# Second cross attention: query products in two pairs, values one a step, the routing's logits at step 9 and positions at 22, read at 23

## The chip, the cores and the metric

The kernel runs as one program on one core of a Trainium2 chip. The metric is the device time of one execution in microseconds (us). All data is float32.

## The reference, cut to what matters

Two transformer decoder layers run over 32 sequences of 100 tokens of width 256, with a context of 361 rows of width 128 for each sequence. The stage that the change touches is the cross attention of layer 1, and with it the routing of the mixture of experts that follows:

```python
# L1 cross attention, 16 heads of 64: q = layernorm(x), kv = ctx_512
qh = (q @ Wq).reshape(B, N, 16, 64).transpose(0, 2, 1, 3)
kh = (kv @ Wk).reshape(B, M, 16, 64).transpose(0, 2, 1, 3)
vh = (kv @ Wv).reshape(B, M, 16, 64).transpose(0, 2, 1, 3)
attn = softmax(einsum('bhnd,bhmd->bhnm', qh, kh) / 8)
x = x + einsum('bhnm,bhmd->bhnd', attn, vh) ... @ Wo + bo
# L1 mixture: routing of each token to 8 of 64 experts
scores = sigmoid(layernorm(x) @ gate.T); sfc = scores + e_bias
# 4 of 8 groups by the sum of their two best, then the 8 best experts;
# weights = scores of the chosen ones, divided by their sum, times 2.5;
# position of a token in its expert's list = how many tokens before it chose that expert (capacity 256)
```

## The kernel before

The whole kernel is five stages in a row; the one here is `packed_cross_attention` (layer 1). It handles two sequences (u = 0, 1) in a **turn**. There are 16 turns of real work, written as one turn of preparation (turn -1), turn 0, a hardware loop over turns 1 to 14, and turn 15. A turn is 26 **steps** (`SLOTS`), and each engine runs through the same 26 steps in its own program; semaphores tie them together. The order of the work is written by hand: tables at the top of the function say at which step a piece is issued.

At every step n the Tensor engine (PE) makes one tile of scores, 128 rows (head and token) by 361 keys, for the tile that is 10 steps ahead (`scores`, L1093), and transposes the probabilities of the tile that is 5 steps ahead in three pieces (`turn_probs`, L1100). The Vector engine (DVE) takes the maximum of the new scores (L1247) and divides the tile that is 9 steps ahead by its sum (reciprocal L1252, scaling L1254). The Scalar engine (ACT) copies the transposed probabilities out of PSUM (`move_probs`, L1198) and makes the exponentials (`exponent`, L1203). Work that is 10 steps ahead passes over into the next turn: from step 16 on, the scores are those of the next turn.

Beside this, single pieces have steps of their own:

- `WEIGH_AT`: probabilities times values, 24 pairs of small products (L1114), at steps 3, 9, 16, 22; `Y_AT`: the output projections y0 at step 13 and y1 at step 24 (L1123), which the Vector engine adds to X (`add`, L1259).
- `X_AT`, `P_AT`, `Q_AT`: for the next turn, the transposed input (step 4), four query projections p0 to p3 (L1057) and four query products with the key weights (L1071). Product j fills two PSUM tiles, q0.j and q1.j, which the Scalar engine copies to `qT` (L1185).
- `V0_AT`, `V1_AT`: the values of the sequences 0 (of the next turn) and 1 (of this turn), six products each (L1082), copied by the Scalar engine (L1192).
- The routing of the turn before this one, woven in: `ROUTED_X` (transposed input, PE L763), `ROUTED_L` (logits, PE L782, moved by the Scalar engine in L790), `ROUTED_C` (positions by counting, PE L867 and L868). The choice of the experts (`choose`) is a chain of some 30 small Vector instructions, cut by `yield` into groups; `CHOOSE_AT` says at which steps a group runs. One group reads the positions out of PSUM (L840 to L842); the last one finds the eight row numbers of each token (L853 to L860), and waits before it for the semaphore `rows_free` (L855), that the rows of the turn before were written.
- GpSimd (POOL) then copies the normalised tokens into the rows (`copy_rows`, L876) and sends 16 indirect writes (`send_row`, L882). `PACE` holds each of them back until the Vector engine has reached a given step; the first `FIRST` of them come before GpSimd's two small norm operations (L227) and the bias addition (L1006), the others after.

All the pieces of the list share two PSUM banks, 6 and 7, through `Ring`: the entries of a turn (30 of them) in order of their steps are dealt in turn to bank 6 and bank 7, and the engine that fills an entry first waits until the entry before it in the same bank has been read out:

```python
def plan(self, names):
    self.bank = {name: n % self.n for n, name in enumerate(names)}
...
def wait_free(self, pe, name, i):
    pe.wait_ge(self.moved[self.bank[name]], self.before(name, i) + 1)
```

So moving one entry changes which pairs of entries follow each other in a bank. Before the change the order is, as step:entry(bank), v for values, q for a query product (two entries):

0:v1.0(6) 1:v1.1(7) 2:v1.2(6) 4:xT(7) 4:v1.3(6) 5:p0(7) 6:v1.4(6) 7:p1(7) 8:v1.5(6) 8:rx(7) 10:rl(6) 11:p2(7) 12:p3(6) 13:y0(7) 14:q0.0(6) 14:q1.0(7) 15:q0.1(6) 15:q1.1(7) 17:v0.0(6) 17:rc(7) 18:v0.1(6) 18:v0.2(7) 19:q0.2(6) 19:q1.2(7) 20:v0.3(6) 21:q0.3(7) 21:q1.3(6) 23:v0.4(7) 24:y1(6) 25:v0.5(7)

Here rx, rl and rc are the routing's transposed input, logits and positions.

## Time and profile before

| | us |
|---|---|
| median of 3 runs (3569.85 to 3587.38) | 3585.91 |
| the profiled execution: its own time | 3585.76 |
| its span | 3584.0 |
| Tensor engine busy | 3278.9 (91%) |
| Vector engine busy | 1882.1 (53%) |
| Scalar engine busy | 1653.5 (46%) |
| GpSimd busy | 783.2 (22%) |

The span is what the profiler covers between the first and the last instruction; the profiled execution's own time is 1.8 us longer. In a timeline, a row is an instruction or a few of one kind: its start in us, its length, the engine, the line, the operation, output and inputs, how many, and in square brackets how long the engine had been idle before it and who ended that. An instruction of the Tensor engine's float32 work shows as two in the counts (x2 for one product). Ends of matmuls are modelled and overlap the start of the next one, so the distance from start to start is what an instruction costs.

### The profile page before, as it was taken

How to read it: one execution, taken by the hardware profiler on the slowest of the kernel's cores; microseconds unless marked ns; L12 is line 12 of the kernel's file. 1: busy time of each engine (PE TensorE's matmuls, PEld its weight loads, DVE VectorE, ACT ScalarE, POOL GpSimd, SP SyncE). 2: the span in 40 equal slices, each digit the busy share in tenths (PEclk: the TensorE clock that was granted, in tenths of full speed). 3: DMA queues.
4: the chain of work that ended last, by engine and by line, in shares of the span. 5: the costliest groups of instructions: out<-in, count | busy, mean ns of one | idle time of the engine just before them, and what ended most of it. 6: DMA issues, size and time to landing. Idle time of an engine off the chain costs nothing. (4 is left out here: it accounts for less than half of the span.)

```text
span 3584.0 us, 76477 instructions
## 1 busy us (share of the span) xinstructions
PE 3278.9 (91%) x24554; PEld 2427.9 (68%) x24555; DVE 1882.1 (53%) x5145; ACT 1653.5 (46%) x4616; POOL 783.2 (22%) x854
## 2 busy tenths in 40 slices
PE   5999999899999898999996979999999999979982
PEld 4777776566666566777775757777677777656761
DVE  3555555577777645222224645665656656543333
ACT  2555555576666511222222336666666666631220
POOL 0000000000000000333331100223233232234774
PEclk9999999899999889999998989999999999989996
DMA  8500000300000042111112010100000000113784
GB/s 268 140 0 0 0 0 2 150 10 10 10 10 10 29 137 75 28 29 32 30 21 51 0 51 10 33 26 21 15 11 13 13 12 15 40 49 106 216 209 138
DMA packets 136402, 181.21 MB, mean 51 GB/s; under 512 B 36156, under 2 KB 108601, under 8 KB 135308
## 3 DMA queue, kind: packets, MB, share of 16 engines
q1 hardware_dynamic: 81810, 131.61, 11.9%
q0 software_dynamic: 45760, 26.67, 4.6%
q10 hardware_dynamic: 8762, 22.01, 1.7%
q8 instruction: 42, 0.69, 0.1%
q14 instruction: 28, 0.23, 0.0%
HBM read 116.11 MB, written 103.61 MB: 61 GB/s over the span
## 5 line engine op out<-in xcount | busy, mean ns | idle before, releaser
L1247 DVE TENSOR_REDUCE e_nmx<-PS 128x1 f32<-128x361 f32 x416 | 221.5, 532 | 400.5 <-PE PS L1093 350.9
L1093 PE MATMUL PS<-e_cT,e_qT 128*128 128x361 f32 x832 | 337.6, 488 | 0.0
L1599 ACT ACTIVATE b_p<-PS,b_nmx 100x361 f32<-100x361 f32 x512 | 267.6, 569 | 149.5 <-DVE b_nmx L1681 149.5
L882 POOL DMA_INDIRECT slot_rows<-r_row,r_rows_now x256 | 256.4, 1002 | 360.4 <-DVE e_p L1254 306.6
L1198 ACT ACTIVATE e_pT<-PS 121x384 f32<-121x384 f32 (+1 forms) x416 | 199.1, 479 | 221.1 <-PE PS L1100 212.4
L2592 PE MATMUL PS<-c_wgu,c_tile_xT 128*128 x912 | 290.0, 461 | 1.2 <-ACT c_tile_xT L2647 1.2
L1100 PEld LDWEIGHTS PS<-ident,e_p 128*121 128x121 f32 x1248 | 199.6, 186 | 105.8 <-issue 10.4
L1681 DVE TENSOR_REDUCE b_nmx<-PS 100x1 f32<-100x361 f32 x512 | 243.8, 526 | 45.6 <-PE PS L1445 45.6
L1203 ACT ACTIVATE e_p<-PS,e_nmx 128x361 f32<-128x361 f32 x416 | 232.7, 559 | 37.0 <-DVE e_nmx L1247 36.9
L1452 PEld LDWEIGHTS PS<-ident,b_p 100*121 100x121 f32 x1536 | 188.2, 185 | 63.0 <-ACT b_pT L1583 32.8
L1452 PE MATMUL PS<-ident,b_p 100*121 100x100 f32 x1536 | 223.0, 280 | 8.4 <-ACT b_pT L1583 6.2
L2592 PEld LDWEIGHTS PS<-c_wgu,c_tile_xT 128*128 128x128 f32 x912 | 169.5, 191 | 77.9 <-issue 2.8
L2848 POOL DMA_INDIRECT sum<-f_y,f_y_token x128 | 199.5, 1559 | 89.1 <-issue 55.2
L1100 PE MATMUL PS<-ident,e_p 128*121 128x128 f32 x1248 | 206.0, 275 | 9.0 <-issue 9.0
L1093 PEld LDWEIGHTS PS<-e_cT,e_qT 128*128 128x128 f32 x832 | 143.5, 191 | 97.6 <-issue 87.5
L1082 PE MATMUL PS<-e_wv,e_cT 128*121 128x512 f32 x384 | 198.9, 601 | 11.4 <-DVE r_key L842 11.3
L517 ACT ACTIVATE a_sm<-a_sm,a_nmx 100x100 f32<-100x100 f32 x512 | 186.0, 368 | 13.9 <-DVE a_nmx L585 13.9
L1254 DVE TENSOR_SCALAR e_p<-e_p,e_rden 128x361 f32<-128x361 f32 x416 | 170.4, 410 | 14.8
L1686 DVE COPY b_pT<-PS 121x300 f32<-121x300 f32 x256 | 120.0, 469 | 95.2 <-PE PS L1452 91.2
L2654 ACT ACTIVATE c_gated<-PS 128x352 f32<-128x352 f32 x114 | 52.9, 464 | 232.5 <-PE PS L2592 231.8
L2612 PE MATMUL PS<-c_wd,c_hT 128*128 x684 | 157.2, 379 | 0.7 <-DVE c_hT L2683 0.7
L1114 PE MATMUL PS<-e_pT,e_v 121*64 121x100 f32 x3072 | 147.3, 252 | 0.4 <-ACT e_pT L1198 0.4
(339 smaller groups left out, 6490.1 us busy)
## 6 DMA issues: line engine op xcount, KB each, us to landing
f_w<-in_f_W SPq DMA_DIRECT2D x64, 384.0 KB
slot_rows<-a_empty SPq DMA_DIRECT2D x1, 21504.0 KB, 65.0
f_xg<-slot_rows SPq DMA_DIRECT2D x64, 336.0 KB
c_wgu<-in_c_GU ACTq DMA_DIRECT2D x8, 1408.0 KB, 16.6
sum<-X SPq DMA_DIRECT2D x2, 3200.0 KB, 57.2
f_sums<-sum SPq DMA_DIRECT2D x16, 400.0 KB
b_cT<-in_ctx_T SPq DMA_DIRECT2D x32, 181.5 KB, 2.3
e_cT<-in_ctx_T SPq DMA_DIRECT2D x32, 181.5 KB, 2.4
```

Of the source, the lines that this page charges most:

```text
L882: pool.indirect_dma_start(out=self.rows, in_=self.row[:, u, :], in_offset=None, out_offset=bass.IndirectOffsetOnAxis(ap=self.rows_now[:, u ...
L1082: mr.fill_done(pe.matmul(mr.at(v_name, KEYS, 512), cT[:, u, c * KEYS:(c + 1) * KEYS], wv[:, n * 512:(n + 1) * 512], start=True, stop=True) ...
L1093: sr.fill_done(pe.matmul(sr.at(f"s{m}", ROWS, CTX), qT[:, at:at + ROWS], cT[:, u, 0:CTX], start=True, stop=True), f"s{m}")
L1100: last = pe.transpose(tr.at(f"p{m}", KEYS, CH, ROWS)[:, c, :], p[:, m % NP, c * KEYS:(c + 1) * KEYS], k.ident[:])
L1198: tr.move_done(act.activation(pT[:, :, at:at + rows], tr.at(f"p{m}", KEYS, CH, ROWS)[:, :, 0:rows], ACT.Copy), f"p{m}")
L1203: sr.move_done(act.activation(p[:, m % NP, 0:CTX], sr.at(f"s{m}", ROWS, CTX), ACT.Exp, bias=nmx[:, m:m + 1], accum_out=den[:, m:m + 1]), f ...
L1247: dve.tensor_reduce(nmx[:, m:m + 1], sr.at(f"s{m}", ROWS, CTX), AX.X, ALU.max, negate=True).then_inc(max_ready, 1)
L1452: last = pe.transpose(tr.at(f"p{g}{a}", KEYS, CH, S)[:, c, :], p[:, g % 2, a, c * KEYS:(c + 1) * KEYS], k.ident[0:S, 0:S])
L1599: sr.move_done(act.activation(p[:, g % 2, a, 0:CTX], sr.at(f"s{g}{a}", S, CTX), ACT.Exp, bias=nmx[:, g, a:a + 1]), f"s{g}{a}")
L1681: dve.tensor_reduce(nmx[:, g, a:a + 1], sr.at(f"s{g}{a}", S, CTX), AX.X, ALU.max, negate=True).then_inc(max_ready, 1)
L2592: last = pe.matmul(banks.at(f"{a}{n}", 128, HALF), xT[:, c, :], wgu[:, bass.ds(now, 1), what, c, n * HALF:(n + 1) * HALF] .rearrange("p o ...
L2848: pool.indirect_dma_start(out=k.sums[n % 2].rearrange("s b d -> (s b) d"), in_=y[:, n % 4, half, :], in_offset=None, out_offset=bass.Indir ...
```

## The change

It edits tables and the order of three things:

- The query projections are at steps 5 to 8 in a row. The query products come as two pairs, at steps 10 and 11 and at steps 17 and 18. No step has two values products any more; v1.4 and v1.5 go to steps 12 and 14.
- The routing's logits are issued at step 9 (before: 10), its positions at step 22 (before: 17). The choice of experts runs at steps 12, 13, 16, 18, 20, 22, 23, 24 and 25 in nine groups: a new `yield` cuts the group that finds the eight best experts. The positions are read at step 23 and the last group runs at step 25.
- `add(1, i)` stands inside step 25, ahead of the last group of the choice. GpSimd's writes are paced by steps 1, 2 and 4 to 17 of the next turn (before: 22 to 25 and 3 to 14), two of them ahead of the norms (before: four).

The stage after this one (`shared_and_experts`) gets one more call of `next` at its step 4, so that the choice of the last turn keeps its places.

```diff
@@ class Routing, choose
         for u in range(2):
             last = dve.max(self.best8[:, u, :], masked[:, u, :])
         link(last)
+        yield
         dve.sem_inc(self.passed, 1)
@@ packed_cross_attention
-    P_AT = {5: 0, 7: 1, 11: 2, 12: 3}
-    Q_AT = {14: 0, 15: 1, 19: 2, 21: 3}
-    V0_AT = {17: (0,), 18: (1, 2), 20: (3,), 23: (4,), 25: (5,)}
-    V1_AT = {0: 0, 1: 1, 2: 2, 4: 3, 6: 4, 8: 5}
-    ROUTED_X, ROUTED_L, ROUTED_C = 8, 10, 17
-    CHOOSE_AT = (12, 13, 14, 15, 16, 18, 19, 20)
-    FIRST = 4
-    PACE = [22, 23, 24, 25] + [SLOTS + n for n in range(3, 15)]
+    P_AT = {5: 0, 6: 1, 7: 2, 8: 3}
+    Q_AT = {10: 0, 11: 1, 17: 2, 18: 3}
+    V0_AT = {15: 0, 19: 1, 20: 2, 21: 3, 23: 4, 25: 5}
+    V1_AT = {0: 0, 1: 1, 2: 2, 4: 3, 12: 4, 14: 5}
+    ROUTED_X, ROUTED_L, ROUTED_C = 8, 9, 22
+    CHOOSE_AT = {12: 1, 13: 1, 16: 1, 18: 1, 20: 1, 22: 1, 23: 1, 24: 1, 25: 1}
+    FIRST = 2
+    PACE = [SLOTS + n for n in (1, 2, *range(4, 18))]
@@ the Vector engine's turn
-                        if prev and n in CHOOSE_AT:
-                            next(choosing, None)
-                    if this:
-                        add(1, i)
+                        if this and n == SLOTS - 1:
+                            add(1, i)
+                        if prev:
+                            for _ in range(CHOOSE_AT.get(n, 0)):
+                                next(choosing, None)
@@ shared_and_experts
-    CHOOSE_AT = {2: 1, 3: 2, 4: 1, 5: 1, 6: 1, 7: 2}
+    CHOOSE_AT = {2: 1, 3: 2, 4: 2, 5: 1, 6: 1, 7: 2}
```

The entries of the two banks now follow each other like this:

0:v1.0(6) 1:v1.1(7) 2:v1.2(6) 4:xT(7) 4:v1.3(6) 5:p0(7) 6:p1(6) 7:p2(7) 8:p3(6) 8:rx(7) 9:rl(6) 10:q0.0(7) 10:q1.0(6) 11:q0.1(7) 11:q1.1(6) 12:v1.4(7) 13:y0(6) 14:v1.5(7) 15:v0.0(6) 17:q0.2(7) 17:q1.2(6) 18:q0.3(7) 18:q1.3(6) 19:v0.1(7) 20:v0.2(6) 21:v0.3(7) 22:rc(6) 23:v0.4(7) 24:y1(6) 25:v0.5(7)

Two places of the Tensor engine's program and one of the Vector engine's show it. Rows are instructions in program order; those without an output are register and wait instructions; "waits" names the semaphores, `bank6_moved` being the count of entries read out of bank 6. Lines of the changed kernel are one higher or one lower than those of the kernel before.

The Tensor engine in the loop, from y0 (step 13) on, before:

```order
L1123 MATMUL PS<-e_wo,e_oT 100x256 [waits bank7_moved]
L1123 MATMUL PS<-e_wo,e_oT 100x256 x7
L87 REGISTER_ALU
L1093 MATMUL PS<-e_cT,e_qT 128x361 [waits bank0_moved]
L87 REGISTER_ALU
L1098 REGISTER_ALU [waits bank4_moved]
L1100 MATMUL PS<-ident,e_p 121x128 [waits e_scaled]
L1100 MATMUL PS<-ident,e_p 121x128 x2
L159 REGISTER_ALU [waits bank7_moved]
L159 REGISTER_ALU [waits bank6_moved]
L1071 MATMUL PS<-e_short,e_wkT 128x200 [waits bank7_moved]
```

The same place now:

```order
L1124 MATMUL PS<-e_wo,e_oT 100x256 [waits bank6_moved]
L1124 MATMUL PS<-e_wo,e_oT 100x256 x7
L87 REGISTER_ALU
L1094 MATMUL PS<-e_cT,e_qT 128x361 [waits bank0_moved]
L87 REGISTER_ALU
L1099 REGISTER_ALU [waits bank3_moved]
L1101 MATMUL PS<-ident,e_p 121x128 [waits e_scaled]
L1101 MATMUL PS<-ident,e_p 121x128 x2
L159 REGISTER_ALU
L1083 MATMUL PS<-e_wv,e_cT 121x512 [waits bank7_moved]
```

Before, a query product stood one step behind y0 and needed the bank of y0; now a values product in the other bank stands there, and the next user of y0's bank is v0.0 at step 15.

The Tensor engine in the loop at the positions (step 17) and the two values products of step 18, before:

```order
L867 MATMUL PS<-r_taken,earlier 100x64
L868 MATMUL PS<-r_before,ones 100x64
L87 ISA
L1093 MATMUL PS<-e_cT,e_qT 128x361 [waits bank2_moved]
L87 REGISTER_ALU
L1098 REGISTER_ALU [waits bank4_moved]
L1100 MATMUL PS<-ident,e_p 121x128 [waits e_scaled]
L1100 MATMUL PS<-ident,e_p 121x128 x2
L159 REGISTER_ALU
L1082 MATMUL PS<-e_wv,e_cT 121x512 [waits bank6_moved]
L159 REGISTER_ALU
L1082 MATMUL PS<-e_wv,e_cT 121x512 [waits bank7_moved]
```

The positions now (step 22), up to the values product of step 23:

```order
L868 MATMUL PS<-r_taken,earlier 100x64
L869 MATMUL PS<-r_before,ones 100x64
L87 REGISTER_ALU
L1094 MATMUL PS<-e_cT,e_qT 128x361 [waits bank1_moved]
L87 REGISTER_ALU
L1099 REGISTER_ALU [waits bank3_moved]
L1101 MATMUL PS<-ident,e_p 121x128 [waits e_scaled]
L1101 MATMUL PS<-ident,e_p 121x128 x2
L159 REGISTER_ALU
L1083 MATMUL PS<-e_wv,e_cT 121x512 [waits bank7_moved]
```

The next user of the positions' bank was the second values product one step later; it is now y1, two steps later.

The Vector engine in the loop at the last group of the choice (step 25) now, up to its first wait for the rows:

```order
L1246 TENSOR_REDUCE e_nmx<-PS 128x1 [waits bank0_filled,r_step]
L105 REGISTER_ALU
L1251 RECIPROCAL e_rden<-e_den 128x1 [waits bank2_moved]
L1252 REGISTER_ALU
L1253 TENSOR_SCALAR e_p<-e_p,e_rden 128x361 [waits e_rden_ready]
L1258 ISA [waits bank6_filled]
L1258 TENSOR_TENSOR X<-X,PS 100x256
L854 MAX r_key<-r_key 100x8 x2
L241 REGISTER_ALU
L857 TENSOR_SCALAR r_row<-r_score 100x2x64 [waits r_rows_free,r_step]
L858 TENSOR_SCALAR r_row<-r_token_f 100x2
```

Before, this group stood at step 20, between two steps of plain softmax work; now it follows the addition of y1 and stands ahead of the next turn's first maximum.

## Rows read from the trace of the kernel before

**Rows 1.** Busy time by engine (count), Tensor clock, DMA share, GB/s: one turn.
```profile
2497.60:2563.34 65.74, 63.45 (x469) 47.06 (x468) 40.03 (x150) 41.06 (x109) 19.48 (x22) 1.00 0.06 16
```
**Rows 2.** Timeline of SP: the routing's store, once a turn, turns 2 and 14.
```profile
2300.39 0.60 SPq L774 DMA_DIRECT2D r_xT_rows<-r_xT  x1
...
3089.25 0.56 SPq L774 DMA_DIRECT2D r_xT_rows<-r_xT  x1
```
**Rows 3.** Groups by line, 14 turns: busy, mean ns | idle before, releasers.
```profile
L1082 PE MATMUL PS<-e_wv,e_cT 128*121 128x512 f32 x338 | 174.2, 597 | 11.3 <-DVE r_key L842 11.3
...
L1071 PE MATMUL PS<-e_short,e_wkT 64*128 64x200 f32 x448 | 53.1, 355 | 20.8 <-DVE X L1259 17.0 <-ACT e_v L1192 3.7
```
**Rows 4.** Timeline of PE, steps 14 and 15 of one turn.
```profile
2511.11 0.49 PE L1100 MATMUL PS<-ident,e_p 128*121 128x128 f32 x3
2512.82 0.95 PE L1071 MATMUL PS<-e_short,e_wkT 64*128 64x200 f32 x8 [1.22 <-DVE X L1259]
...
2514.41 0.49 PE L1100 MATMUL PS<-ident,e_p 128*121 128x128 f32 x3
2514.83 0.95 PE L1071 MATMUL PS<-e_short,e_wkT 64*128 64x200 f32 x8
```
**Rows 5.** Timeline of DVE: the addition of y0 in that turn.
```profile
2512.36 0.41 DVE L1259 TENSOR_TENSOR X<-X,PS 100x256 f32 x1
```
**Rows 6.** Timeline of PE: the two values products of step 18.
```profile
2522.61 1.02 PE L1082 MATMUL PS<-e_wv,e_cT 128*121 128x512 f32 x2
2524.44 1.12 PE L1082 MATMUL PS<-e_wv,e_cT 128*121 128x512 f32 x2 [0.81 <-DVE r_key L842]
```
**Rows 7.** Timeline of DVE: the last of three reads of the positions.
```profile
2524.09 0.29 DVE L842 TENSOR_SCALAR r_key<-PS 100x128 f32<-100x128 f32 x1
```
**Rows 8.** Timeline of PE, step 21: the last query product.
```profile
2529.80 0.49 PE L1100 MATMUL PS<-ident,e_p 128*121 128x128 f32 x3
2530.56 0.95 PE L1071 MATMUL PS<-e_short,e_wkT 64*128 64x200 f32 x8 [0.27 <-ACT e_v L1192]
```
**Rows 9.** Timeline of ACT: copies of query products (two each) and of values.
```profile
2513.80 0.90 ACT L1185 ACTIVATE e_qT<-PS 128x400 f32<-128x400 f32 x2 [1.12 <-PE PS L1071]
...
2515.86 0.90 ACT L1185 ACTIVATE e_qT<-PS 128x400 f32<-128x400 f32 x2
...
2529.92 0.59 ACT L1192 ACTIVATE e_v<-PS 121x512 f32<-121x512 f32 x1
...
2544.92 0.60 ACT L1192 ACTIVATE e_v<-PS 121x512 f32<-121x512 f32 x1
```
**Rows 10.** Timeline of PE: values at steps 25 and 0, with no wait.
```profile
2542.00 1.02 PE L1082 MATMUL PS<-e_wv,e_cT 128*121 128x512 f32 x2
2542.86 0.77 PE L1093 MATMUL PS<-e_cT,e_qT 128*128 128x361 f32 x2
...
2543.79 1.02 PE L1082 MATMUL PS<-e_wv,e_cT 128*121 128x512 f32 x2
```
**Rows 11.** Timeline of DVE: last group's start (step 20), y1's addition, step 0's maximum.
```profile
2529.76 0.35 DVE L853 MAX8 r_key<-r_key 100x8 f32<-100x64 f32 x2
...
2542.84 0.41 DVE L1259 TENSOR_TENSOR X<-X,PS 100x256 f32 x1
2543.67 0.53 DVE L1247 TENSOR_REDUCE e_nmx<-PS 128x1 f32<-128x361 f32 x1 [0.42 <-PE PS L1093]
```
**Rows 12.** Single lines over the span: ns min/median/max, first and last start.
```profile
L876 POOL COPY r_row<-r_xn x16: 607/609/612, 2267.8 to 3230.5; 100x512 f32<-100x512 f32 x16
...
L882 POOL DMA_INDIRECT slot_rows<-r_row,r_rows_now x256: 985/992/1143, 2271.6 to 3251.5; - x128
...
L1254 DVE TENSOR_SCALAR e_p<-e_p,e_rden x416: 406/408/523, 2137.6 to 3181.5; 128x361 f32<-128x361 f32 x139
```
**Rows 13.** Timeline of PE in turn 15: after the loop's exit, and at the positions.
```profile
3155.71 1.00 PE L1100 MATMUL PS<-ident,e_p 128*121 128x128 f32 x3 [8.99 <-issue]
...
3181.47 0.45 PE L867 MATMUL PS<-r_taken,earlier 100*100 100x64 f32 x2 [2.14 <-DVE r_before L830]
```

More of the change, by code:

```diff
@@ L950, in packed_cross_attention @@
         order += [(n, 2, f"q{r}.{j}") for n, j in Q_AT.items() for r in range(HT)]
-        order += [(n, 3, f"v0.{m}") for n, ms in V0_AT.items() for m in ms]
+        order += [(n, 3, f"v0.{m}") for n, m in V0_AT.items()]
         led = [name for _, _, name in order]
@@ L1143, in turn @@
                         if nxt and n in V0_AT:
-                            for m in V0_AT[n]:
-                                values(0, m, i + 1)
+                            values(0, V0_AT[n], i + 1)
                         if this and n in V1_AT:
@@ L1227, in turn @@
                         if nxt and n in V0_AT:
-                            for m in V0_AT[n]:
-                                move_values(0, m, i + 1)
+                            move_values(0, V0_AT[n], i + 1)
                         if this and n in V1_AT:
```

## The prediction

> **What bounds the kernel now.** I read the busy table of single turns first. In a turn of 65.74 us the Tensor engine is busy for 63.45 at clock 1.00 (the upper of its two levels, 2.4 GHz), the Vector engine for 40.0, the Scalar engine for 41.1 and GpSimd for 19.5 [rows 1]. So the Tensor engine sets the pace of this stage, and only what makes it stand still is to be had; all its products stay the same in number. Then the timeline of SP shows that the turns are equal: its store comes once a turn, and from the one at 2300.39 to the one at 3089.25 are twelve turns, 788.86 / 12 = 65.74 us [rows 2]. One turn can stand for the 14 of the loop. Then the groups by line, over 14 turns: the Tensor engine is idle ahead of three pieces alone. It waits 17.0 us for the addition of y0, 11.3 us for the read of the positions and 3.7 us for a copy of values [rows 3], 32.0 us in all, 2.3 us a turn.
>
> Last, the timelines of one turn tell why, and what each costs from start to start.
>
> - **First wait, step 14.** The transposes start at 2511.11; the query product behind them would start 0.42 later, as it does one step on (2514.41 to 2514.83), so at 2511.53. It starts at 2512.82, **1.29 us late** [rows 4]: its bank held y0, and the addition of y0 began at 2512.36 [rows 5]. The bank opened 0.46 us after that start.
> - **Second wait, step 18.** A values product takes 0.86 us (2542.00 to 2542.86), the scores and transposes of the next step 0.93 (to 2543.79), so a plain step with values is 1.79 [rows 10]. The first of step 18 starts at 2522.61, so the second was due at 2523.47 and came at 2524.44, 0.97 late [rows 6]. What follows a wait also runs 0.1 us longer (1.12 against 1.02), which makes **1.07 us**. It waited for the Vector engine's third read of the positions, which began at 2524.09 [rows 7]; the bank opened 0.35 us after that start.
> - **Third wait, step 21.** The query product comes at 2530.56 and was due at 2529.80 + 0.42 = 2530.22, **0.34 us late** [rows 8], behind a copy of values that began at 2529.92 [rows 9]. So a bank opens 0.64 us after the start of such a copy.
>
> The three are 2.70 us a turn.
>
> **The change, part by part.** Each entry moved is a question to the two banks: does the entry ahead of it in its bank leave in time?
>
> *The first wait goes.* Behind y0 now stands v1.5 in the other bank; in the old clock it starts between 2511.11 and 2511.53, and its own bank was last held by v1.4 at step 12, long copied. The bank of y0 is next wanted by v0.0, one values step (1.79) later, so at 2512.90 or after. It opens by 2512.82 as before, in time: gain 1.29.
>
> *The second wait goes, and half of it threatens to come back.* The positions, at step 22, are read at step 23. The next user of their bank is y1 at step 24. From the values product of step 23 to y1 the Tensor engine needs the same 1.79 us. The third read began 1.48 us after the values product of its step (2522.61 to 2524.09) and frees the bank 0.35 later: 1.83. So y1 is some 0.04 us late, and pays perhaps the 0.1 of a restart. From below the cost is nothing (the old pattern to 0.04 exactly), from above 0.34, the size of the smallest wait that exists now. I take 0.14, since the two sums differ by less than the rounding of three rows. Gain 1.07 less 0.14.
>
> *The third wait goes; two close pairs come.* q3 now follows q2 in both banks, and q1 follows q0. From one query product to the next are 2.01 us (2512.82 to 2514.83) [rows 4]. The Scalar engine's copies of the first begin 0.98 us after it where it is free (2513.80) and 1.03 us where its exponential is ahead (2514.83 to 2515.86) [rows 9]. The second copy begins 0.45 later; a copy of 400 columns is some 0.09 shorter than one of 512, so the bank opens 0.55 after that: 1.03 + 0.45 + 0.55 = 2.03. That is 0.02 late, twice a turn; before, the same pair at steps 14 and 15 shows no wait, which is the lower end; the upper end is 0.34 each. I take 0.03 each. Gain 0.34 less 0.06.
>
> *Logits at step 9, values at 12, 14, 15, 19, projections in a row.* The closest are v1.4 and v0.1, one step behind a query product, 2.01 less some 0.1 later; they want the bank of its first tile, open after 1.03 + 0.55 = 1.58. All others have more between them and the entry ahead in their bank. They cost nothing; what hides them is the Scalar engine's slack of 24 us a turn, and if it were gone, each late copy would cost its lateness.
>
> *The Vector engine's groups.* The positions' chain must be ready at step 22: its last piece runs at step 20. The crowded place is now the turn's end: addition of y1 (0.41), then the last group (2529.76 until the rows' copy could start at 2530.76, 1.00), then the maximum of step 0. The addition starts at 2542.84, so the maximum comes at 2544.25 instead of 2543.67, 0.58 later [rows 11]. Behind it wait the exponential and the copy of v1.0, which began 1.25 after the maximum (2544.92) [rows 9]; its bank would open at 2544.25 + 1.25 + 0.64 = 2546.14. It is wanted by v1.2, two values steps after v1.0, at 2543.79 + 3.58 = 2547.37 [rows 10]. There are 1.2 us to spare; cost nothing.
>
> *GpSimd and SP.* The copy of the rows and 16 writes move by some 5 to 7 steps; a write takes 0.99 us [rows 12] and the pace gives it a step of 1.79 or more. The last leaves at step 17; `rows_free` is wanted at step 25, over 15 us later. The norms behind two writes are ready by about step 4 and wanted at 6 and 8. The context loads on SP wait for the same steps as before. Cost nothing.
>
> So a turn of the loop gains 2.70 - 0.14 - 0.06 = 2.50 us, 14 turns **35.0 us**. Turn 0 has the first wait but no routing: it gains **1.3**. In turn 15 the Tensor engine stands 2.14 us before the positions [rows 13]; asked five steps later, they are there: take **2.1**, between 5 (the tail behind them moves up too) and, on the other side, a loss of 2.6. That loss would come from the stop of 8.99 us after the loop's exit [rows 13]: unpaced writes of GpSimd run through it, 12 before and 14 now, at 1.3 us each. The turn of preparation has the same pieces: 0, give or take 1.
>
> Sum: 35.0 + 1.3 + 2.1 = 38.4 us off the profiled execution's own 3585.76, which is within 0.2 of the median of the runs: **3547 us**.
>
> **A rule against it.** The rows' copy is 607 to 612 ns in all 16 cases, the Vector engine's scaling 406 to 408 at the median and 523 at most in 416 [rows 12], whether or not GpSimd works beside it. So neither is held for long now. The Trainium skill (SBUF — State Buffer, Who interferes with whom) says that GpSimd and a Vector instruction in a two-port mode share one port pair as a lock, and that a tensor_scalar can take such a mode; by that rule the copy and the first writes, which now fall on the crowded steps 0 to 2, would stop the scalings there. The trace does not agree so far, the longest case being 0.12 us over the median. What it would make is the second rival.
>
> **The rivals.** A measurement of this kernel can tell about 0.5% (18 us) from no change.
>
> 1. *Close pairs wait.* y1 and the two second query products each wait 0.34 us, as a values copy causes now, instead of 0.20 together: 14 x 0.82 = 11.5 us back, **3558 us**. For it: the margins are within 0.05 us of nothing. Against it: the same pair at steps 14 and 15 runs without a wait.
> 2. *The turn's end is too crowded.* If the copy (0.61) and the two writes at steps 1 and 2 (0.99 each) each held up a scaling, the Vector engine would be 2.6 us later than worked out, 1.4 beyond the 1.2 to spare, and v1.2 or what follows it would stand: 14 x 1.4 = 20 us back, **3567 us**; with the first rival on top 3578, no change. Against it: the flat durations above.
> 3. *Slower: the last group waits for the rows.* It waits for `rows_free` in the Vector engine's own order, with the next turn's maxima behind it. If the 16 writes of the turn before are not landed by step 25, every us of lateness goes into every turn. It decides from the 63rd us of the turn on; to be slower than before by 18 us it needs 56 / 14 = 4 us beyond that, so writes that end some 20 us later than their pace. Price at 5 us: 3547 + 70 = **3617 us**. Against it: a write takes 0.99 us and steps are longer.
>
> That the change does not do what it says can be left out: the printed order shows each piece at its new place.
>
> **How the numbers follow.** The forecast has 0.78, the first rival 0.10, the second 0.08 (half of it inside 0.5%), the third 0.04. Faster by over 0.5% is 0.78 + 0.10 + half of the second, less 0.05 for runs that scatter (the three before lie 17 us apart): 0.87. Within 0.5%: 0.09. Slower: 0.04. The range reaches down to 3530, since one run before was 16 us below the median and turn 15 may give 3 more, and up to 3563, past the first rival with the loss of turn 15.
>
> **What would show it.** In the changed profile SP's stores should come every 63.2 us (63.0 to 63.6). The groups by line should show no idle time before query products for the addition of X and none before values products for the positions' read; before the output projection (now L1124) up to 0.15 us a turn. y0's addition and the maxima of step 0 should start as worked out. A period above 64.0 us, idle time of the Tensor engine at steps 2 to 4, or a wait of the Vector engine ahead of the last group would make it wrong.

## The result, and the profile after

The kernel before took 3584.31 us (median of 7 runs, 3569.85 to 3593.34), the changed one 3555.81 us (7 runs, 3545.51 to 3558.3): a ratio of 0.9916, 95% interval 0.9899 to 0.9933. It is faster by 0.84%, beyond the 0.5% that can be told from no change. Forecast were 3547 us and a range of 3530 to 3563. The profiled execution took 3556.59 us, its span is 3554.8: 29.2 less than before, where 38.4 were expected. The sum is short by some 9 us, and most of it turned out to sit in one place of the loop.

One turn, from store to store, answers to [rows 1]. The columns are those of that view.

```profile
2487.34:2551.24 63.90, 63.52 (x468) 47.30 (x466) 40.95 (x150) 40.73 (x109) 19.42 (x22) 1.00 0.06 16
```

SP's stores, turns 2, 3, 7, 8 and 14, answer to [rows 2]:

```profile
2295.72 0.60 SPq L774 DMA_DIRECT2D r_xT_rows<-r_xT  x1
2359.59 0.56 SPq L774 DMA_DIRECT2D r_xT_rows<-r_xT  x1
...
2615.14 0.56 SPq L774 DMA_DIRECT2D r_xT_rows<-r_xT  x1
2679.90 0.56 SPq L774 DMA_DIRECT2D r_xT_rows<-r_xT  x1
...
3063.25 0.56 SPq L774 DMA_DIRECT2D r_xT_rows<-r_xT  x1
```

A turn takes 63.87 to 63.95 us, one (turn 7) takes 64.76. Against 65.74 that is 1.85 a turn, where 2.50 were forecast. In turn 7 a values product starts 0.83 us late behind a copy of the Scalar engine (the 0.7 in the first row below); why that copy was late was not followed up. The Tensor engine's groups by line in the loop, which answer to [rows 3], say what is left of its idle time (busy us, mean ns | idle before, releasers):

```profile
L1083 PE MATMUL PS<-e_wv,e_cT 128*121 128x512 f32 x328 | 167.9, 593 | 0.7 <-ACT e_qT L1185 0.7
L1115 PE MATMUL PS<-e_pT,e_v 121*64 121x100 f32 x2644 | 129.2, 251 | 5.0 <-issue 5.0
L1124 PE MATMUL PS<-e_wo,e_oT 128*100 128x256 f32 x446 | 102.0, 382 | 0.0
...
L1072 PE MATMUL PS<-e_short,e_wkT 64*128 64x200 f32 x448 | 53.0, 355 | 0.2 <-ACT e_qT L1185 0.2
```

The waits for the addition of y0, for the positions' read and for the values' copy are gone (20.8 and 11.3 us in [rows 3]). Something new stands ahead of the weighing: 5.0 us whose releaser is "issue", so the engine waited for no other engine and no transfer that the profile shows. The timeline of the Tensor engine shows it at step 3:

```profile
2535.27 0.49 PE L1101 MATMUL PS<-ident,e_p 128*121 128x128 f32 x3
2535.69 2.10 PE L1115 MATMUL PS<-e_pT,e_v 121*64 121x100 f32 x43
2538.17 0.44 PE L1115 MATMUL PS<-e_pT,e_v 121*64 121x100 f32 x5 [0.38 <-issue]
2538.55 0.87 PE L1094 MATMUL PS<-e_cT,e_qT 128*128 128x361 f32 x2
```

From the weighing's start to the next scores are 2.86 us; without a gap it is 2.21 (the weighing of step 22, 2518.10 to 2520.31). So the **gap costs 0.65 us**, more than the 0.38 that is shown as idle. It stands after some 43 of the 48 products in each of the turns 2 to 14, and not in turn 1, which is entered without the loop's jump: 13 times 0.65 = 8.5 us. [rows 3] has no idle time of this kind.

What GpSimd and the Vector engine do there: the last group of the choice, the loop's jump, maxima with no wait ahead of them, and two of GpSimd's writes, 0.32 us before the weighing starts and 0.99 us into it.

```profile
2535.37 1.00 POOL L883 DMA_INDIRECT slot_rows<-r_row,r_rows_now  x1 [4.10 <-DVE e_p L1253]
2536.68 1.01 POOL L883 DMA_INDIRECT slot_rows<-r_row,r_rows_now  x1 [0.30 <-issue]
2537.72 0.73 POOL L227 TENSOR_TENSOR r_rstd<-r_var,minus_half 100x2 f32<-100x2 f32 x1
```

```profile
2529.66 0.35 DVE L854 MAX8 r_key<-r_key 100x8 f32<-100x64 f32 x2
...
2531.09 0.53 DVE L1246 TENSOR_REDUCE e_nmx<-PS 128x1 f32<-128x361 f32 x1 [0.34 <-issue]
...
2533.35 0.53 DVE L1246 TENSOR_REDUCE e_nmx<-PS 128x1 f32<-128x361 f32 x1
...
2534.31 0.53 DVE L1246 TENSOR_REDUCE e_nmx<-PS 128x1 f32<-128x361 f32 x1
...
2536.53 0.53 DVE L1246 TENSOR_REDUCE e_nmx<-PS 128x1 f32<-128x361 f32 x1
```

The places where the kernel before put its writes are far from it: one 5.4 us before that weighing, the next 2.7 us after its start.

The stage as a whole, from its first product to the first of the next stage, took 1076.4 us (2118.17 to 3194.53) and takes 1046.3 (2115.99 to 3162.30). Ahead of the stage, where the change touches nothing, 2.2 us were won; behind it, where it touches one table of `shared_and_experts`, some 3 were lost. No run separates that table from scatter.

### The profile page after: what moved, and what is told of

Same layout as the page of the kernel before. It is cut to its first block and busy times, and to the rows that moved or that the text cites. A ratio compares the mean times of both kernels' runs of the same rounds, so it can differ in the third digit from the quotient of the medians.

```text
span 3554.8 us, 76489 instructions
## 1 busy us (share of the span) xinstructions
PE 3279.1 (92%) x24554; PEld 2431.7 (68%) x24555; DVE 1893.1 (53%) x5145; ACT 1646.6 (46%) x4616; POOL 782.5 (22%) x854
## 5 line engine op out<-in xcount | busy, mean ns | idle before, releaser
L1253 DVE TENSOR_SCALAR e_p<-e_p,e_rden 128x361 f32<-128x361 f32 x416 | 183.7, 442 | 14.8
```

## The experiments

The question was what makes the gap. At the start there were three theories: C, the Vector engine's lateness at the turn's end leaves the Tensor engine too little lead; F, the gap belongs to a place in the Tensor engine's program; P, it comes from GpSimd's writes. The runs were made in three groups, each on another chip: 1 to 4, then 5 to 7 with 11, then 8 to 10 with 12. The kernel before, run beside them, took 3577.58 us (one run), 3551.93 us (one run) and 3559.79 us (median of 9). All other times are of one run where no number of runs is given. Periods are the mean over twelve turns, from SP's stores. The changed kernel itself was not run beside experiments 1 to 4; that their chip can show the gap is known from experiment 3.

**1. The last group a step earlier.**

```diff
-    CHOOSE_AT = {..., 24: 1, 25: 1}
+    CHOOSE_AT = {..., 24: 2}
```

> The changed kernel with the last group of the choice at step 24, beside the group before it, instead of at step 25; the Tensor engine's program is the same. To be explained: the changed kernel's stores come every 63.89 us and not every 63.2, and of the 0.69 us a turn that are missing 0.65 lie in one place, an idle time of 0.38 us (releaser: issue) inside the weighing of step 3, in turns 2 to 14 alone. Theory C (crowd): the Vector engine is about 1 us late at steps 25 to 3, since the last group and the loop's jump now stand together ahead of step 0's maximum, so what the Tensor engine's queue waits for comes with too little lead, and it runs dry in the densest stretch. Then the gap goes, the store comes every 63.24 us (63.89 - 0.65), about 9 us less in all. Theory F (layout): the gap belongs to a place in the Tensor engine's program, whatever the Vector engine does: period stays 63.89. Theory P (GpSimd): the gap comes from the writes and norms at steps 1 to 3: stays, or moves by a step.

Measured: 3543.68 us, period 63.24, no gap in any turn. The writes moved with the Vector engine: they now begin 1.32 us before the weighing (2539.38) and at it.

```profile
2539.38 2.28 PE L1115 MATMUL PS<-e_pT,e_v 121*64 121x100 f32 x48
```
```profile
2538.06 1.00 POOL L883 DMA_INDIRECT slot_rows<-r_row,r_rows_now  x1 [6.18 <-DVE e_p L1253]
2539.42 0.99 POOL L883 DMA_INDIRECT slot_rows<-r_row,r_rows_now  x1 [0.36 <-issue]
```

The Tensor engine's program is that of the changed kernel, so F does not hold by itself. But two things changed at once, lateness and the time of the writes.

**2. Both last groups at step 25.**

```diff
-    CHOOSE_AT = {..., 24: 1, 25: 1}
+    CHOOSE_AT = {..., 25: 2}
```

> The changed kernel with the last two groups of the choice at step 25 (1.5 us more of Vector work ahead of step 0's maximum). The Tensor engine's program is the same. Theory C (crowd): the gap in the weighing of step 3 grows by up to the 1.5 us, or waits for the Vector engine appear beside it; period 64.5 or more. Theory F (layout): gap of 0.38 us at the same place, period 63.9, unless the maxima become so late that they are waited for by name. Theory P: as F.

Measured: 3553.51 us, period 64.26, and no gap in the weighing. The Tensor engine waits at step 2, and loses time once more in the transposes behind the weighing:

```profile
2528.57 0.77 PE L1094 MATMUL PS<-e_cT,e_qT 128*128 128x361 f32 x2
...
2533.74 1.12 PE L1083 MATMUL PS<-e_wv,e_cT 128*121 128x512 f32 x2 [0.49 <-ACT e_v L1192]
2534.70 0.77 PE L1094 MATMUL PS<-e_cT,e_qT 128*128 128x361 f32 x2
2535.31 0.49 PE L1101 MATMUL PS<-ident,e_p 128*121 128x128 f32 x3
2535.73 2.28 PE L1115 MATMUL PS<-e_pT,e_v 121*64 121x100 f32 x48
2537.94 0.88 PE L1094 MATMUL PS<-e_cT,e_qT 128*128 128x361 f32 x2
2538.65 0.75 PE L1101 MATMUL PS<-ident,e_p 128*121 128x128 f32 x3
2539.24 0.51 PE L1047 MATMUL PS<-ident,e_xn 100*128 100x100 f32 x4
```

The wait is v1.2 behind the copy of v1.0, the chain that the second rival named. The maximum of step 0 (2531.98) comes 3.41 us after its scores; in the changed kernel it is 1.80 (2529.29 to 2531.09), before it was 0.81 (2542.86 to 2543.67, [rows 10, 11]). v1.2 was due 0.33 us after the transposes of its step (2532.76) and came 0.98 after them: 1.61 us more lateness made it 0.65 late, so 0.96 us were still to spare in the changed kernel.

**The gap is not gone here, it has moved.** From the transposes to the next piece are 0.59 us, where experiment 1 has 0.32 (2542.30 to 2542.62): 0.27 us lost. It is 0.33 in turn 1, 0.50 in turn 2 and 0.57 to 0.61 from turn 3 on. The Tensor engine's weight loads show the stop, here and in the changed kernel:

```profile
2539.03 0.18 PEld L1101 LDWEIGHTS PS<-ident,e_p 128*121 128x121 f32 x1 [0.19 <-issue]
```
```profile
2538.14 0.28 PEld L1115 LDWEIGHTS PS<-e_pT,e_v 121*64 121x64 f32 x5 [0.54 <-issue]
```

The writes begin 0.53 and 1.84 us into the weighing (2536.26 and 2537.57), 0.85 later than in the changed kernel, and the load behind the stop comes 0.85 later as well (3.30 us after the weighing's start against 2.45). It comes 1.46 us after the start of the second write in both kernels. So the stop follows the writes and not a place in the program. The period adds up: 63.24 + 0.65 for the wait + 0.10 for the longer product behind it + 0.27 = 64.26. Against C speaks only that the loss became smaller (0.27 for 0.65) with a later Vector engine; experiment 4 decides it.

**3. The kernel before with the turn's end alone.**

```diff
-    CHOOSE_AT = (12, 13, 14, 15, 16, 18, 19, 20)
-    FIRST = 4
-    PACE = [22, 23, 24, 25] + [SLOTS + n for n in range(3, 15)]
+    CHOOSE_AT = (12, 13, 14, 15, 16, 18, 19, 25)
+    FIRST = 2
+    PACE = [SLOTS + n for n in (1, 2, *range(4, 18))]
...
+                        if this and n == SLOTS - 1:
+                            add(1, i)
                         if prev and n in CHOOSE_AT:
                             next(choosing, None)
-                    if this:
-                        add(1, i)
```

> The kernel before with one part of the change alone: y1's addition inside step 25 and the last group of the choice at step 25 behind it, and GpSimd's writes paced as in the changed kernel. Tables of query products, values and positions are those of before, so the Tensor engine's program is that of the kernel before. Theory C (crowd): the gap of the step 3 weighing appears here too: period 65.74 + 0.65 = 66.4, some 9 us more in all. Theory F (layout): no gap, period 65.74. Theory P: gap appears, as with C.

Measured: 3579.66 us, period 66.26, 0.52 above the kernel before. The gap is there, in the same place, in turns 2 to 14, with the Tensor engine's program unchanged:

```profile
2543.78 2.10 PE L1114 MATMUL PS<-e_pT,e_v 121*64 121x100 f32 x43
2546.14 0.44 PE L1114 MATMUL PS<-e_pT,e_v 121*64 121x100 f32 x5 [0.26 <-issue]
```
```profile
2543.38 1.00 POOL L882 DMA_INDIRECT slot_rows<-r_row,r_rows_now  x1 [4.10 <-DVE e_p L1254]
2544.69 1.01 POOL L882 DMA_INDIRECT slot_rows<-r_row,r_rows_now  x1 [0.31 <-issue]
```

The writes begin 0.40 us before the weighing and 0.91 into it, nearly as in the changed kernel, and the weight load behind the stop (2546.11) comes 1.42 us after the second of them. F falls.

**4. All of GpSimd's writes later.**

```diff
-    FIRST = 2
-    PACE = [SLOTS + n for n in (1, 2, *range(4, 18))]
+    FIRST = 0
+    PACE = [SLOTS + n for n in range(4, 20)]
```

> The changed kernel with GpSimd's sixteen writes paced by steps 4 to 19 of the next turn and all of them behind the norms: nothing but the copy of the rows and two small norms is left for GpSimd in steps 0 to 3. Theory P (GpSimd): the gap of the step 3 weighing goes, period 63.24. Theories C and F: the gap stays, period 63.89. In all cases the Vector engine's scalings of steps 1 to 4 should be back at 0.41 us where no write runs beside them (0.61 and 0.65 in the changed kernel).

Measured: 3541.05 us, every turn 63.19 to 63.26 but the last of the loop (65.10), no gap in the weighing. The Vector engine is exactly as late as in the changed kernel: its maximum of step 3 begins 0.85 us into the weighing (2530.58 to 2531.43), there it was 0.84 (2535.69 to 2536.53). So lateness without the writes makes no gap: **C falls, the early writes are needed**. (The norms also start earlier here, since no write stands ahead of them; no run moves the writes and leaves the norms.) The scalings of steps 1 to 4 are back below 0.45 us, as expected; further on in the turn, beside other writes, some of 0.46 to 0.68 remain.

The loss came back at another place. All 16 writes behind the loop's exit now run unpaced, and the Tensor engine has "issue" stops of 5.26, 2.76 and 4.18 us there. From the store of turn 14 to the next stage are 104.76 us, against 98.24 in experiment 1 and 99.05 in the changed kernel. Over the whole stage this version takes 1044.4 us, experiment 1 takes 1035.8 and the changed kernel 1046.3. So of the two ways to take the gap out of the loop only experiment 1's pays on such a chip; the total of 3541.05 us does not show it, since it was not taken beside the 3555.81.

With experiment 2 taken for a case without a stop, the four together gave a narrower theory, D: a write that begins about 1.0 us into this weighing (or 0.3 us before it) holds up the Tensor engine's instructions. Three runs were to tell which one, and whether the Vector engine has a part in it.

**5 to 7. One early write; two writes a step earlier; on time, but with a write in the weighing.**

```diff
@@ 5: the changed kernel
+    FIRST = 1
+    PACE = [SLOTS + n for n in (1, *range(4, 19))]
@@ 6: the changed kernel
+    PACE = [SLOTS + n for n in (0, 1, *range(4, 18))]
@@ 7: experiment 1, GpSimd's turn
-                    send(j, range(FIRST), early)
                     if routed_next:
                         layer_norm_rstd(pool, r.ln, j + 1)
                     if led:
                         layer_norm_rstd(pool, ln, j + 4)
+                    send(j, range(FIRST), early)
```

> The changed kernel with one of GpSimd's writes ahead of the norms instead of two, at the same pace (step 1), the others paced by steps 4 to 18. The Vector and the Tensor engine's programs are the same, the Vector engine is as late at the turn's end as in the changed kernel. So far the gap in step 3's weighing was there where the Vector engine was late and a write began 0.9 to 1.0 us after the weighing's first product (and another 0.3 to 0.4 before it), and it was gone both with the last group at step 24 (writes 1.3 before and at 0.0) and with all writes later. Theory D (a write against the Tensor engine's instruction supply): a write in a short stretch of time holds the fetching of the Tensor engine's next instructions after the loop's jump; the Vector engine's lateness does nothing but bring the second write into that stretch. The write 1.0 us after the start is the guilty one; it is gone here: gap gone, period 63.24. If instead the write at -0.3 is the guilty one, the gap stays, period 63.89. Theory C (crowd, lateness of the Vector engine alone): the gap stays, 63.89.

> The changed kernel with GpSimd's first two writes paced by steps 0 and 1 instead of 1 and 2: by the lag from scaling to write (about 1.0 us) they begin some 2.6 and 0.3 us before the weighing of step 3, and none 1.0 us into it. Theory D with the second write guilty: gap gone, period 63.24. Theory D with the write at -0.3 guilty, or theory C (late Vector engine alone): gap stays, period 63.89.

> The kernel with the last group at step 24 (Vector engine on time, no gap, period 63.23), with GpSimd's two early writes behind its two norm operations instead of ahead of them: the first then begins some 1.1 us after the weighing's first product, the second 1.3 later. Theory D: the gap comes back in turns 2 to 14 although the Vector engine is on time, period 63.6 to 63.9. Theory C: no gap, period 63.23.

Measured: 3519.16, 3511.01 and 3509.13 us, all with a period of 63.19 and no gap. Read alone, the first two look like D and the third speaks against it. But no kernel of this group had any "issue" time on the Tensor engine behind the loop's exit either, where [rows 13] has 8.99 us. This needed a control on the same chip.

**8 to 10. The changed kernel again, with 6 and 7 beside it.**

> The changed kernel as it is, once more, as the control on the same chip as the three beside it: in the last four runs no kernel had an idle time with the releaser issue, neither in step 3's weighing nor behind the loop's exit, and the kernel before took 3552 us there and not 3578 to 3586. Theory K (chip): how fast a chip supplies instructions differs, and the gap is found on some chips alone; then here it is either 63.89 us a turn with stops behind the loop's exit, or 63.2 with none. All theories otherwise: 63.89.

> The changed kernel with GpSimd's first two writes paced by steps 0 and 1, beside its control. It counts only if the control shows the gap. Theory D (a write about 1.0 us into the weighing holds the Tensor engine's instruction supply): no gap, 63.24. Theory C (lateness of the Vector engine alone), or D with the write at -0.3 guilty: gap stays, 63.89.

> Last group at step 24 (Vector engine on time) and the two early writes behind the norms, the first some 1.1 us into the weighing of step 3. It counts only if the control shows the gap. Theory D: gap in turns 2 to 14, period 63.6 to 63.9. Theory C: no gap, 63.23.

Measured: the changed kernel 3518.52 us (5 runs, 3508.69 to 3524.59) against 3559.79 before (9 runs), ratio 0.988, interval 0.9859 to 0.9902; the two others 3526.43 and 3510.89 us. The period is 63.19 in all three. In the changed kernel the writes are where they were, 0.33 us before the weighing and 0.97 into it, the maxima just as late, and there is no gap:

```profile
2473.13 2.28 PE L1115 MATMUL PS<-e_pT,e_v 121*64 121x100 f32 x48
2475.34 0.87 PE L1094 MATMUL PS<-e_cT,e_qT 128*128 128x361 f32 x2
```
```profile
2472.80 0.99 POOL L883 DMA_INDIRECT slot_rows<-r_row,r_rows_now  x1 [4.10 <-DVE e_p L1253]
2474.10 1.02 POOL L883 DMA_INDIRECT slot_rows<-r_row,r_rows_now  x1 [0.30 <-issue]
```

So the observation behind theory K holds: **the same program with the same writes has the gap in one profile and not in another**. That the chip makes the difference, as K says, is not shown: the record does not name the chip of the first profile, and no chip was used in two sessions, so anything else that differed between the sessions would look the same. The difference stays from execution to execution: seven runs of 3545.51 to 3558.3 us there, five of 3508.69 to 3524.59 here. Runs 5 to 7 and the two repeated here say nothing for or against D: on these two chips no kernel shows what they were to take away.

**11. The positions' part alone.**

```diff
-    ROUTED_X, ROUTED_L, ROUTED_C = 8, 10, 17
-    CHOOSE_AT = (12, 13, 14, 15, 16, 18, 19, 20)
+    ROUTED_X, ROUTED_L, ROUTED_C = 8, 10, 22
+    CHOOSE_AT = (12, 13, 14, 15, 16, 23, 24, 25)
```

> The kernel before with the part on the positions alone: positions at step 22, read at step 23, the two groups behind at steps 24 and 25, y1's addition ahead of the last one; GpSimd's writes all behind the norms at steps 4 to 19, so that they can't meet the weighing of step 3. Query products and values stay where they were. All theories: the wait for the positions' read (1.07 us) goes, the waits for y0's addition (1.29) and for the values' copy (0.34) stay, y1 is some 0.1 late: period 65.74 - 1.07 + 0.14 = 64.8. If the parts were not additive, it would lie off that by more than 0.1.

Measured: 3538.7 us, period 64.42, 0.38 below what was expected. The wait of 1.22 us before the query product of step 14 is there as before, the positions' wait is gone, and the wait of step 21 is gone as well, although the same entries follow each other in the banks. The copy of v0.3 starts 1.06 us after its product (2454.50 to 2455.56); before, it was 1.58 (2528.34 to 2529.92), because an exponential ahead of it had waited 0.50 us for the Vector engine's maximum. So the third wait came from the choice's groups at steps 19 and 20, which are empty now; that is read from these rows, and no run moves those two groups alone. With it: 65.74 - 1.07 - 0.34 + 0.11 = 64.44.

**12. A version with all of it.**

```diff
-    ROUTED_X, ROUTED_L, ROUTED_C = 8, 9, 22
-    CHOOSE_AT = {12: 1, 13: 1, 16: 1, 18: 1, 20: 1, 22: 1, 23: 1, 24: 1, 25: 1}
-    FIRST = 2
-    PACE = [SLOTS + n for n in (1, 2, *range(4, 18))]
+    ROUTED_X, ROUTED_L, ROUTED_C = 8, 9, 21
+    CHOOSE_AT = {12: 1, 13: 1, 16: 1, 18: 1, 20: 1, 21: 1, 22: 1, 23: 1, 24: 1}
+    FIRST = 0
+    PACE = [SLOTS + n for n in range(4, 20)]
```

> A version to beat the changed kernel: positions at step 21 and read at step 22, so that y1 (0.11 us late in the changed kernel, 0.18 with its restart) has a step more; the last group at step 24, so that the Vector engine is on time at the turn's end; all of GpSimd's writes at steps 4 to 19, behind the norms. Expected period 63.89 - 0.65 - 0.18 = 63.06 where the chip shows the gap, and 63.19 - 0.13 = 63.06 where it does not; against its control 9 to 12 us less where the gap is, 2 to 3 us less where it is not.

Measured: 3513.26 us (4 runs, 3512.53 to 3513.96), ratio to the kernel before 0.9875, interval 0.9858 to 0.9892; the period is 63.03. y1 now starts 0.33 us after the transposes and takes 3.45 to the next scores; in the changed kernel on the same chip it was 0.44 and 3.53:

```profile
2491.90 0.49 PE L1101 MATMUL PS<-ident,e_p 128*121 128x128 f32 x3
2492.23 3.62 PE L1124 MATMUL PS<-e_wo,e_oT 128*100 128x256 f32 x16
2495.68 0.77 PE L1094 MATMUL PS<-e_cT,e_qT 128*128 128x361 f32 x2
```
```profile
2460.96 0.49 PE L1101 MATMUL PS<-ident,e_p 128*121 128x128 f32 x3
2461.40 3.70 PE L1124 MATMUL PS<-e_wo,e_oT 128*100 128x256 f32 x16
2464.93 0.77 PE L1094 MATMUL PS<-e_cT,e_qT 128*128 128x361 f32 x2
```

The period is 0.16 us shorter than that of the changed kernel, 2.3 us over 14 turns. In the medians it is 5.3 us ahead of the changed kernel, but the two intervals cover each other: beaten in the trace, not in the time. It was not run on a chip with the gap. There its period should gain 0.65 us a turn more, some 9 us, but its writes are paced as in experiment 4, which lost 5.7 us at the loop's exit against the changed kernel, so the net gain is open.

## Why the prediction was right, and where not

**The three waits** were read rightly and all went. On a chip without the gap the period is 63.19, 2.55 us below the 65.74 of the kernel before, which was profiled in the first session alone; forecast were 2.50 and 63.2. The medians there lie 41 us apart, against 38.4.

**y1 at step 24** was the closest call: worked out at 0.04 late, costed at 0.14. It starts 0.44 instead of 0.33 us after the transposes and costs 0.11 + 0.08 = 0.19 a turn. **The close pairs:** q3 comes 0.07 late (2510.23 to 2510.72, 0.49 against 0.42), q1 not at all (0.42); forecast 0.06 for both. The first rival priced these three waits at 1.02 us together and falls: they cost 0.26.

**The third wait** was there in size, but its cause was only half read: the copy of values was late because of the Vector engine's groups (experiment 11). There it goes with the positions' part alone, so it did not need the new places of the query products.

**The Vector engine at the turn's end** is 0.99 us later at step 0's maximum, not 0.58. What was left out is the loop's jump: an idle time of 0.34 us <-issue stands there now, which before fell into a wait for the Tensor engine. To spare were 1.2 by the sum; 0.96 us remain at 0.99 late (experiment 2). The step was mis-sized and by itself still cost nothing; but GpSimd's writes are paced by the Vector engine, and its lateness is what put them beside the weighing (experiment 1).

**The step that failed inside a right forecast is "GpSimd and SP. Cost nothing".** It looked at what GpSimd delivers and when its queue is free, and not at what else a write meets. In the changed kernel's profile its two early writes and the weighing of step 3 cost 13 x 0.65 = 8.5 us. 3547 + 8.5 = 3555.5, and 3555.81 was measured; that the two agree so closely is chance, since turn 7 lost 0.8 us, the parts ahead of and behind the stage changed by 2 to 3 us, and the runs lie 13 us apart. The prediction had named "a period above 64.0 or idle time at steps 2 to 4" as signs against it: the period stayed at 63.9, the idle time came, at step 3.

**The second rival** was right in the place (GpSimd's early writes, steps 0 to 3) and wrong in the mechanism. Scalings are held now: the longest is 757 ns, where [rows 12] has 523, and the two beside the bias addition and the write of step 4 take 0.61 and 0.65 us.

```profile
2540.10 0.61 DVE L1253 TENSOR_SCALAR e_p<-e_p,e_rden 128x361 f32<-128x361 f32 x1
...
2542.25 0.65 DVE L1253 TENSOR_SCALAR e_p<-e_p,e_rden 128x361 f32<-128x361 f32 x1
```
```profile
2539.10 1.40 POOL L1007 TENSOR_TENSOR X<-X,e_bo 100x256 f32 x2
2541.70 1.04 POOL L883 DMA_INDIRECT slot_rows<-r_row,r_rows_now  x1 [1.20 <-DVE e_p L1253]
```

By the Trainium skill (SBUF — State Buffer, Who interferes with whom) this is what a shared port would do, and here the trace agrees with it; but the Vector engine stands idle for 0.9 us ahead of the maximum between them, so nobody waits.

The prediction took the flat durations of [rows 12] as evidence against holding, "whether or not GpSimd works beside it". They were not. What decides is when in a write the scaling begins. In the changed kernel 63 scalings last over 0.45 us beside a write; they begin 0.48 to 0.71 us after the write's start and end 1.15 to 1.21 us after it. Eight that begin in that part, and all that begin earlier or later in a write, take their 0.41. In the kernel before 122 scalings overlap a write and not one begins between 0.45 and 0.75 us after its start. So the hold could not show there, and moving the writes brought it out.

**The third rival**, the wait for the rows, did not occur: the last group began 0.32 us after y1's addition did (2529.34 to 2529.66), with no wait ahead.

**Turn 15.** The wait of 2.14 us before the positions is gone, as forecast. In its place y1 waits 1.20 us for the positions' read at the same place where the loop pays 0.11; turn 15 has no products of a next turn between the two, which would explain it:

```profile
3156.63 3.67 PE L1124 MATMUL PS<-e_wo,e_oT 128*100 128x256 f32 x16 [1.20 <-DVE r_key L843]
```

At the loop's exit stand eleven "issue" stops, 5.3 us together, between 3123 and 3136, beside unpaced writes, instead of one of 8.99. They are the smaller part of what the exit costs:

```profile
3125.00:3140.00 15.00, 10.77 (x34) 6.86 (x35) 3.40 (x11) 3.32 (x10) 6.93 (x7) 0.54 0.04 7
```

The columns are those of [rows 1]. The granted clock falls to 0.54 of full speed in this stretch, so mostly to the lower of the two levels, after the Tensor engine had been stopped again and again; the scores at 3137.11 take 1.41 us instead of 0.77. From the store of turn 14 to the next stage are 99.05 us (before: 105.28). In its second profile the changed kernel has none of these stops, the clock stays at 1.00 and the same way takes 86.52 us. So in the first profile this part cost 12.5 us more, and the gap 8.5. The kernel before has its stop of 8.99 us in the same part, so the forecast, which counts from there, loses nothing by it: it had feared up to 2.6 us more here, and the part became 6.2 us shorter.

## What to carry to other kernels

When several waits of one engine are taken out, look at what its idle time had also been covering: here, as far as can be read, the supply of its own instructions, in the densest stretch behind a loop's jump, at the same moment as another engine's indirect writes. A queue that "has time" is not thereby free to move, and moving it may only move the loss: the writes of experiment 4 left the loop's steps alone and met the loop's exit. And run the changed kernel itself beside an experiment that takes an effect away: five runs here could not speak, because their chips did not show the effect.

## What the runs showed of the hardware that was not expected

- **The same program ran differently in two profiles.** One program with its writes at the same place (0.33 before and 0.97 us into the weighing, against 0.32 and 0.99) takes 63.19 us a turn in one and 63.90 in the other, and "issue" stops of the Tensor engine behind the loop's exit are found in all kernels of the first group and in none of the other eight. The kernel before is faster on those chips as well (3552 and 3560 against 3578 and 3584 us), but was not profiled there. Whether the chip is the cause is open (experiments 8 to 10).
- **Where the gap shows, it goes with early writes of GpSimd** (experiments 1 to 4). Starts 0.32 to 0.40 us before the weighing and 0.91 to 0.99 us into it: a gap near its end, 0.65 and 0.52 us. Starts at 0.53 and 1.84: 0.27 us lost in the transposes behind it. Starts at -1.32 and 0.04, or none: no loss. Where there is a stop, it ends 1.42 to 1.46 us after the second write's start and 2.73 to 2.77 after the first's; the two are always 1.31 us apart, so which of them does it is open. That the instructions are what is late is argued from the releaser, and not shown: the profile lists two queues of kind "instruction" (42 and 28 packets over the span) and not when each packet ran. The Trainium skill (Runtime: NRT & Kernel Launch, Instruction fetch mechanics) says that each engine's sequencer fetches its program in blocks by a DMA queue of its own, and that a taken jump breaks this prefetch where its target lies outside the blocks at hand. That would fit a gap that is missing in turn 1 and stands in the same place in all turns behind a jump, and no row here proves it.
- **A write holds a scaling only in a part of its 0.99 us.** Scalings that begin 0.48 to 0.71 us after its start are stretched from 0.41 to as much as 0.68 us; those that begin 0.35 to 0.45 us or 0.8 us and more after it are not (changed kernel, 63 stretched ones; in experiment 12 the latest stretched one begins 0.83 us after the start).
- **The lag of a paced write:** from the end of the scaling that releases it to the start of the write are 0.97 us (step 1: 2533.99 + 0.41 = 2534.40 to 2535.37), so its place can be chosen only in steps of the Vector engine, plus this.
